# A spectral, spiking and mixture-of-experts layer on one core: synthesis loads moved ahead, block copies moved to GpSimd, one padding tile less

## The reference, cut to what matters

```python
x = x + conv(ln(x))        # spectral convolution on the sphere
t = t + shift_unit(ln(t))  # opcode unit: one-hot nibbles, shifts
x = x + spikes(ln(x))      # q, k, v through spiking neurons, linear attention, output projection
t = t + experts(ln(t))     # top 2 of 8 gated experts

def conv(x):               # x: 8 x 32 x 64 x 128, 32 latitudes as channels, 64 x 128 as the sphere
    xf = rfft(x) * (sqrt(2 pi) / 128)
    x_ft = einsum('lmj,bcjm->bclm', P_ANA, xf)
    top = einsum('bixy,ioxy->boxy', x_ft[:, :, :32, :32], w1)   # w1, w2 complex, 32 x 32 x 32 x 32
    bot = einsum('bixy,ioxy->boxy', x_ft[:, :, -32:, :32], w2)
    g = einsum('lmj,bclm->bcjm', P_SYN, concat(top, bot)) / sqrt(2 pi)
    return irfft(g) * 128
```

## Time and profile before

| what | us |
|---|---|
| median of 3 runs | 1301.36 |
| lowest, highest | 1296.43, 1301.63 |
| the profiled execution's own time | 1295.22 |
| its span | 1293.4 |
| busy: PE, DVE, ACT, POOL | 993.2, 859.4, 654.1, 564.4 |

### The profile page before, as it was taken

One profiled execution on the slowest core, in us unless ns is written; L12 is line 12 of the kernel. 1 busy time (PEld: TensorE's weight loads), 2 busy tenths in 40 slices (PEclk: granted clock), 3 DMA queues, 4 the chain that ended last, 5 costly groups with the idle time before them and its releaser, 6 DMA issues. The chain is left out here.

```text
span 1293.4 us, 23831 instructions
## 1 busy us (share of the span) xinstructions
PE 993.2 (77%) x6645; PEld 837.2 (65%) x6646; DVE 859.4 (66%) x2743; ACT 654.1 (51%) x1400; POOL 564.4 (44%) x731
## 2 busy tenths in 40 slices
PE   9847746876677675867666453099999999999997
PEld 7837644654456464746555342088888888888886
DVE  7707633756579898888984765066766766667665
ACT  3427732454868877687755431044444444444443
POOL 3310000121132575656665667535555555555554
PEclk9978977976878978778787655599999999999999
DMA  9997966940010010000000001111111111111110
GB/s 264 227 248 156 240 171 157 271 103 20 20 50 20 20 47 19 30 16 20 25 12 30 22 19 35 60 33 35 42 46 50 48 50 42 46 48 47 49 37 2
DMA packets 111924, 93.12 MB, mean 72 GB/s; under 512 B 8012, under 2 KB 100556, under 8 KB 111081
## 3 DMA queue, kind: packets, MB, share of 16 engines
q1 hardware_dynamic: 83753, 62.28, 20.5%
q0 software_dynamic: 9088, 17.33, 4.1%
q10 hardware_dynamic: 19008, 12.59, 3.8%
HBM read 55.61 MB, written 38.39 MB: 73 GB/s over the span
## 5 line engine op out<-in xcount | busy, mean ns | idle before, releaser
L1721 POOL DMA_INDIRECT out_dram<-res,index x156 | 155.8, 999 | 217.8 <-DVE res L1787 189.8
L1830 ACT ACTIVATE sil<-ps_h 128x512 f32<-128x512 f32 x156 | 93.1, 597 | 254.8 <-PE ps_h L1882 254.8
L1752 DVE TENSOR_TENSOR act_rows<-ps_h,sil 128x512 f32<-128x512 f32 x156 | 108.0, 692 | 133.4 <-ACT sil L1830 133.4
L1901 PE MATMUL ps_y<-r_raw,aT 128*128 x1248 | 164.8, 275 | 0.0
L1901 PEld LDWEIGHTS ps_y<-r_raw,aT 128*128 128x128 f32 x1248 | 151.6, 192 | 0.1
L160 POOL DMA_INDIRECT slots<-x_sb,r_pos x128 | 129.3, 1010 | 47.7 <-issue 36.0
L1880 PE MATMUL ps_h<-r_raw,uTh 128*128 x312 | 137.6, 441 | 1.6 <-DVE uTl L1746 1.6
L1881 PE MATMUL ps_h<-r_raw,uTh 128*128 x312 | 124.7, 400 | 0.0
L1882 PE MATMUL ps_h<-r_raw,uTl 128*128 x312 | 123.0, 394 | 0.0
L1092 PE MATMUL ps_q<-wqkv,zT 128*128 128x256 f32 x256 | 114.1, 537 | 0.0
L1204 POOL TENSOR_TENSOR x_sb<-x_sb,sy 128x256 f32<-128x256 f32 x64 | 43.8, 684 | 137.1 <-ACT sy L1340 136.9
(11 more groups left out here) (242 smaller groups left out, 2468.7 us busy)
## 6 DMA issues: line engine op xcount, KB each, us to landing
slots<-zero SPq DMA_DIRECT2D x4, 2652.0 KB, 23.2
pay<-slots SPq DMA_DIRECT2D x39, 272.0 KB, 2.8
coefc<-coefficients ACTq DMA_DIRECT2D x16, 256.0 KB, 6.2
mixed<-mo ACTq DMA_DIRECT2D x16, 256.0 KB, 9.1
gin<-mixed SPq DMA_DIRECT2D x16, 256.0 KB, 14.7
r_raw<-in_L_ffn_W SPq DMA_DIRECT2D x8, 508.0 KB
out_dram<-res,index POOLq DMA_INDIRECT x156, 2.2
pana<-in_legendre_analysis SPq DMA_DIRECT2D x1, 2048.0 KB, 12.8
```

Of the source, the lines that this page charges most:

```text
L1721: nc.gpsimd.indirect_dma_start(out_rows, bass.IndirectOffsetOnAxis(at, 0), res[:, m % RES, :], None, bounds_check=TOKENS - 1, oob_is_err=F ...
L1752: nc.vector.tensor_tensor(act_rows[:, k], ps_h[:, k, :, DFF:], sil[:, k], ALU.mult).then_inc(s_act, 1)
L1830: nc.scalar.activation(sil[:, k], ps_h[:, k, :, 0:DFF], ACT.Silu).then_inc(s_sil, 1)
L1901: ins = nc.tensor.matmul(dst, aT[:, k, (2 * e + h) * P:(2 * e + h + 1) * P], raw[:, 4 + h, col], start=(h == 0), stop=(h == 1))
```

## The change

It has four parts.

1. In the mixing block GpSimd does the plain copy of the upper half for every degree, with a semaphore `s_sp` of its own; PE and the coefficient loads wait for it too. ACT keeps the negated and the swapped copy.
2. `lw`, `psyn` and `gin` are loaded in the mixing block. They are allocated on the other side of SBUF (`late`), and `gin` now lies in the first slot of `wc`, which is free after chunk 5. SP issues `lw` and `psyn` behind the last late weights, waits for six chunks to be multiplied and stored and loads their degrees of `gin` (rows 0 to 23 of each group of 32, four transfers), waits for all stores and loads the rest (rows 24 to 31, four transfers). The first Legendre product waits for all of `gin`.
3. `pay` is cut in two; at the end of the spike stage `gap_of(6)` and the first part stand ahead of `route_deviation(7)`.
4. The expert stage works through `USED_TILES` = 155 tiles: the last turn has 11.

```diff
+USED_TILES = NTILES + PAIRS - 1
...
-        wc = sb("wc", [P, WS, O, LW, M], at=both)
+        wc = sb("wc", [P, WS, O, LW, M], at=late, side="right")
...
+            psyn = sb("psyn", [P, M, P], at=late, side="right")
+            lw = sb("lw", [P, 4, C], at=late, side="right")
+            gin = wc[:, 0].rearrange("p o l m -> p (o l m)").rearrange("p (j r m o) -> p j r m o", j=4, r=RB, o=16)
...
+            EARLY = 6
+
+            def load_mixed(eng, l0, l1, s):
+                for op in range(2):
+                    for half in range(2):
+                        p0 = op * 64 + half * L2
+                        src = mixed[op].rearrange("l (j h r) f -> h l j (r f)", j=4, h=2)[half, l0:l1]
+                        eng.dma_start(gin[p0 + l0:p0 + l1].rearrange("p j r m o -> p j (r m o)"), src).then_inc(s, 16)
...
                     for n in range(WS * LW // LQ, NCH):
                         sp.wait_ge(s_mm, n - WS * LW // LQ + 1)
                         load_late(sp, n)
-
+                    sp.dma_start(lw[:, :, :], t["L1_conv_lin_w"].rearrange("i d c -> d i c")).then_inc(s_load, 16)
+                    sp.dma_start(psyn[:, :, :], t["legendre_synthesis"].rearrange("p (m q) -> p m q", m=M)).then_inc(s_psyn, 16)
+                    sp.wait_ge(s_mm, EARLY)
+                    for k in range(2):
+                        sp.wait_ge(s_mw[k], STORED * EARLY // 2)
+                    load_mixed(sp, 0, EARLY * LQ, s_gin[0])
                     for k in range(2):
                         sp.wait_ge(s_mw[k], STORED * NCH // 2)
+                    load_mixed(sp, EARLY * LQ, L2, s_gin[1])
...
                     nc.gpsimd.memset(sblk[:, 1], 0.0).then_inc(s_zero, 1)
+                    pool.wait_ge(s_zero, 2)
+                    for n in range(NCH):
+                        k = n % 2
+                        pool.wait_ge(s_cc[k], n // 2 * 32 + 32)
+                        need(pool, s_mm, n - 1)
+                        for l in range(LQ):
+                            dst = sblk[64:96, k, l, :, RB:2 * RB].rearrange("p (q m) f -> p q m f", q=M // MQ)
+                            ins = nc.gpsimd.tensor_copy(dst, coefc[64:96, k, :, l])
+                            if l % 2:
+                                ins.then_inc(s_sp, 1)
...
                         need(act, s_sa, 2 * (n - 1))
+                        need(act, s_sp, 2 * (n - 1))
...
-                            nc.scalar.activation(dst[0:32], src, ACT.Copy)
...
                         pe.wait_ge(s_sa, 2 * n + 1)
+                        pe.wait_ge(s_sp, 2 * n + 1)
...
-                sp.dma_start(lw[:, :, :], t["L1_conv_lin_w"].rearrange("i d c -> d i c")).then_inc(s_load, 16)
-                sp.dma_start(psyn[:, :, :], t["legendre_synthesis"].rearrange("p (m q) -> p m q", m=M)).then_inc(s_psyn, 16)
                 sp.dma_start(einv[:, :], t["fourier_inverse"]).then_inc(s_einv, 16)
-                for j in range(4):
-                    for op in range(2):
-                        for half in range(2):
-                            src = mixed[op].rearrange("l (j h r) f -> j h l (r f)", j=4, h=2)[j, half]
-                            p0 = op * 64 + half * L2
-                            sp.dma_start(gin[p0:p0 + L2, j].rearrange("p r m o -> p (r m o)"), src).then_inc(s_gin[j], 16)
...
                 pe.wait_ge(s_psyn, 16)
+                pe.wait_ge(s_gin[0], 16 * 4)
+                pe.wait_ge(s_gin[1], 16 * 4)
                 for n in range(M):
                     j, at = n // (M // 4), n % (M // 4)
-                    if at == 0:
-                        pe.wait_ge(s_gin[j], 16 * 4)
...
                 add_output(pool, NP2 - 1, LAST)
+                gap_of(pool, NP2 - 2)
+                pay_power(pool, NP2 - 2)
                 route_deviation(pool, NP2 - 1)
-                gap_of(pool, NP2 - 2)
-                pay(pool, NP2 - 2)
+                pay_shares(pool, NP2 - 2)
                 scatter(pool, NP2 - 2, 0, NT)
...
-                    for m in range(STEPS):
+                    for m in range(STEPS - SPARE if last else STEPS):
```

More of the change, by code:

```diff
@@ L106, in build, with sb @@
     with ExitStack() as ctx:
-        def sb(name, shape, dt=F32, at=ctx):
-            return at.enter_context(nc.sbuf_tensor(name, shape, dt))
+        def sb(name, shape, dt=F32, at=ctx, side=None):
+            return at.enter_context(nc.sbuf_tensor(name, shape, dt, side=side))
         def pb(name, shape, dt=F32, at=ctx):
@@ L125, in build @@
         s_par = sem("norm_parameters_loaded")
-        mixed = spectral_conv(nc, t, sb, pb, sem, x_sb, ident, minus_half, x_view, routing, par_rows, s_par)
+        late = ExitStack()
+        mixed, loaded = spectral_conv(nc, t, sb, pb, sem, x_sb, ident, minus_half, x_view, routing, par_rows, s_par, late)
         routing.allocate(sb)
         with ExitStack() as a:
-            weights = synthesis_and_weights(nc, t, sb, pb, sem, ident, minus_half, a, mixed, par_rows, s_par, routing)
+            weights = synthesis_and_weights(nc, t, sb, pb, sem, ident, minus_half, a, loaded, par_rows, s_par, routing)
+            late.close()
             opcode_and_spikes(nc, t, sb, pb, sem, x_sb, ident, minus_half, weights, slots, routing)
@@ L414, in spectral_conv @@
             s_sa = sem("m_upper_blocks")
+            s_sp = sem("m_upper_plain_rows")
             s_mh = sem("m_first_degrees_mixed")
@@ L548, in _ @@
                         pe.wait_ge(s_sa, 2 * n + 2)
+                        pe.wait_ge(s_sp, 2 * n + 2)
                         need(pe, s_ea, n)
                         half_mixed(n, 1).then_inc(s_mm, 1)
-    return mixed
+    return mixed, (psyn, lw, gin, s_psyn, s_gin, s_load)
 def split3(nc, chain, parts, x, rest):
@@ L561, in split3, with synthesis_and_weights @@
     return nc.vector.tensor_tensor(parts[2], rest, parts[1], ALU.subtract)
-def synthesis_and_weights(nc, t, sb, pb, sem, ident, minus_half, keep, mixed, par_rows, s_par, routing):
+def synthesis_and_weights(nc, t, sb, pb, sem, ident, minus_half, keep, loaded, par_rows, s_par, routing):
+    psyn, lw, gin, s_psyn, s_gin, s_load = loaded
     wqkv = sb("wqkv", [P, 3 * C], at=keep)
@@ L1209, in gap_of, with pay_power @@
             nc.gpsimd.tensor_tensor(gap[:, :], top[:, 1], top[:, 0], ALU.subtract).then_inc(s_gap, 1)
-        SHARE_LINKS = 5
+        SHARE_LINKS, POWER_LINKS = 5, 3
         def pay(pool, v):
+            pay_power(pool, v)
+            pay_shares(pool, v)
+        def pay_power(pool, v):
             chain = Chain(pool, s_share, v * SHARE_LINKS)
@@ L1223, in pay, with pay_shares @@
             chain.link(nc.gpsimd.tensor_tensor(share[:, 0, :], total[:, :], inverse[:, :], ALU.pow))
+            assert chain.n == POWER_LINKS
+        def pay_shares(pool, v):
+            chain = Chain(pool, s_share, v * SHARE_LINKS + POWER_LINKS)
             chain.link(nc.gpsimd.tensor_tensor(share[:, 1, :], power[:, :], share[:, 0, :], ALU.mult))
@@ L1229, in pay @@
                 .then_inc(s_paid, 1)
-            assert chain.n == SHARE_LINKS
+            assert chain.n == SHARE_LINKS - POWER_LINKS
         def deviation(pool, n):
@@ L1629, in experts @@
     TURNS = SLOT_TILES // STEPS
+    SPARE = SLOT_TILES - USED_TILES
     out_rows = out.rearrange("b h w c -> (b h w) c")
@@ L1735, in _ @@
                 turn(TURNS - 1, last=True)
-                for m in range(3):
-                    scatter(TURNS, m - 3)
+                for m in range(USED_TILES - 3, USED_TILES):
+                    scatter(*divmod(m, STEPS))
             @block.vector
@@ L1812, in _ @@
                 turn(TURNS - 1, last=True)
-                for m in range(2):
-                    first_part(TURNS, m - 2)
-                    result(TURNS, m - 2)
+                for m in range(USED_TILES - 2, USED_TILES):
+                    first_part(*divmod(m, STEPS))
+                    result(*divmod(m, STEPS))
             @block.scalar
@@ L1932, in _ @@
                 turn(TURNS - 1, last=True)
-                n = SLOT_TILES
+                n = USED_TILES
                 at_out = [pe.snap(r, min_val=0, max_val=(E - 1) * C) for r in behind]
-                turn_gated(n - 1, 1)
-                expert_out(n - 2, 0, at_out[4:6])
-                expert_out(n - 1, 1, at_out[6:8])
+                turn_gated(n - 1, (n - 1) % 2)
+                for m in (n - 2, n - 1):
+                    q = m % G
+                    expert_out(m, m % 2, at_out[2 * q:2 * q + 2])
 _CONSTANTS = spectral_tables()
```

15 lines of the change are left out of this document (6 added, 9 removed).

## The result

The kernel after takes 1314.46 us (median of 4 executions, 1313.28 to 1315.43); the kernel before, timed beside it, 1299.85 (1296.43 to 1301.63). The ratio is 1.0124, 95% interval 1.0097 to 1.0151: slower by 16 us, 13 to 20 (the two medians lie 14.6 apart). The forecast was 1311.5 us, 10.3 more than before, with 14 of them from the moved loads. The profiled execution of after took 1315.43 us with a span of 1313.5.

What follows compares the result with a forecast made beforehand. Barrier-closed stages bound the kernel one behind another; mixing ends on weight transfers, synthesis waits on loads. Moved loads +14, powers -1, tile -2.7, copies hidden: +10.3 on 1301.4, some 1311.5 us; range 1293 to 1318.

Steps and rivals of the forecast that it cites:

- the base of the sum, 1301.4: Whole kernel before: median of its three runs, 6.1 us above the profiled execution, to which +10.3 was added.
- the term of +14: Synthesis loads moved into the mixing stage: first Legendre product at 216.3 instead of 202.4; term range -4 to +17.
- so 193: End of mixing: chunk 7's store lands 9.1 us after 184, with SP's last four transfers issued by then.
- the 197.8: Mixing stage: 24-row transfers end at 196.5, plus 1.3 us for chunk 7's store; the last four follow.
- 216.3: Start of synthesis: the 8-row transfers, 1.05 MB at 57 GB/s, take 18.5 us and release the first Legendre product.
- Rivals 1 and 2: Synthesis loads: few-row transfers run as fast as 32-row ones, 1294.7, chance 0.2; engine count limits, 1302.5, chance 0.18.
- costed at nothing (+1, hidden by part 2): GpSimd's plain copies in mixing: relieving ACT gains nothing, stage +1 us (-1 to +7), hidden by the moved loads.
- the 29 feared: Mixing stage: 32 POOL copies of 0.9 us, each holding DVE throughout, add 29 us to DVE's 54.3.
- Rival 3: Mixing stage: POOL's copies stretch it until it is DVE's, chunk 7 up to 7 us later, 1316; chance 0.1.
- Part 3, forecast -1: End of spike stage: powers ahead of the last deviation bring scatters 4.1 us earlier, less +2 and +1; range -3.5 to 0.
- the forecast of +2 and +1: End of spike stage: two more scatters under DVE's wide subtractions cost +2; last payload beside DVE's placing +1.
- Part 4, forecast -2.7: Expert stage: dropping the padding tile saves one PE tile period, -2.7 us (-2.5 to -3).

Runs made afterwards that it cites:

- the second: The kernel before, unchanged, profiled once more beside the others: 1299.51 us, ratio 0.9996 (0.9985 to 1.0008).

## Why the prediction was right, and what was mis-sized

**The direction, the place and the mechanism** were as forecast: PE's first Legendre product waits for the 8-row transfers, chunk 7 stays (171.46 against 171.44), a tile of the experts goes. Only the DMA share was read otherwise than forecast: 0.5 to 0.6 and not near 1, with 57 to 70 GB/s where 50 to 60 were expected. The time fell 3 us above the forecast, in its range. The change itself cost 16 us (13 to 20) and not 10.3; that the time came so near owes a part to the base of the sum, 1301.4, which lay above the later medians of the same kernel.

**Part 2, the term of +14, measured +18.3 between the profiles and +20 (15 to 25) alone.** Its steps:
- The table was expected in by 178; issued at 165.33, it landed 12.5 us later, at 178. The 24-row transfers had 170 GB/s forecast, 167 measured (window 184 to 188).
- The step that failed is the landing of chunk 7's store: "so 193", from a median of 9.1 us, which mixes stores beside the weights (7.8 to 10.7 us) with two on idle engines (2.6). It took 17.6 us, to 199.9. The sum had given the store its 1.3 us of DMA time, and not seen that it would land only when SP's early transfers are nearly through. The last four loads wait for it: +2 us on the 197.8 at which they were to start. The kernel with the table alone moved shows the other side, 2.6 us for the same store.
- From the issue of the last four to the first product it took 20.8 us (199.93 to 220.69) and not 18.5. At 57 GB/s their 1.05 MB need 18.4; the rest is probably the way of the first packets (no byte moves from 200 to 201 us) and the 0.13 MB of the inverse Fourier table, which share the engines. No run separates the two. With the store's 2 us that makes 220.7 where the sum had 216.3.
- The first profile of before had its product at 202.40, later than the second (199.88), because chunk 7 ran slowly and its weights came late. That hid some 2 us of the loss in the comparison of the two profiles: against the second one it is 20.8 us.

**Rivals 1 and 2 are out.** Few rows are not as fast as 32, and the number of engines is not it: 8 engines moved 57 GB/s to 8 rows side by side and 196 to 210 to 8 rows spread out, 16 engines 110 GB/s to 16 rows. The Trainium skill's rule in SBUF — State Buffer, Door 1: The DMA port swizzle, by which a transfer reaches only the ports on which its partitions lie, at some 27 GB/s each, is borne out in all five cases. Estimates from that figure, with the measured rates beside them: 8 ports for 32 rows (218, 227 measured), 6 for 24 (163, 167), 4 for 16 (109, 110), 2 for 8 (54, 57 to 63), and 8 for the spread ones (218, 196 to 210). The Trainium skill's rule in DMA: Bandwidth & Descriptors, Why a DMA increments its semaphore by 16 and not by 1, is seen in the shares, 0.75 for 24 rows and 0.5 for 8: it decides how many engines are busy. That the busy ones then wait for the ports is the first rule's reading; what the runs show is 7 GB/s from each of the eight with the rows side by side and 25 with them spread. The forecast had expected a share near 1 for 8 rows, though its own second rival named the eight engines.

**Part 1, costed at nothing (+1, hidden by part 2).** A copy took 0.73 us, where 0.9 was the estimate. DVE lost 10.5 us and not the 29 feared, and had the room. Rival 3 is out. Alone the part measured -1 us (-3 to +1): it is not shown to be a gain. If it is one, it may come by way of the clock in chunk 7, which the forecast did not have.

**Part 3, forecast -1, measured -1.9.** The first scatter comes 5.1 us earlier (13.4 instead of 18.5 us behind the last addition) and not 4.1: gap and powers took 4.9 us in their new place, beside DVE's statistics, instead of 6.06 beside its placing, so the deviation came 0.5 us later and not 1.7. The price was near the forecast of +2 and +1: the scatters lie under DVE's wide subtractions (+1.7 us), and the last payload takes 1.5 us more.

**Part 4, forecast -2.7, measured -3.0** in the pair of profiles and -2.6 in the median.

**The execution that the sum starts from.** Forecast on the median of before, 1301.4; the later medians of the same kernel are 1299.0 to 1300.8. Of the 16 us of the ratio the parts alone explain 20 - 1 - 2 - 2.6 = 14, within their intervals.

## What to carry to other kernels

Before moving a load ahead, see how many rows it fills and where they lie: cutting it by rows, to start with what is ready, can cost more than the idle time it fills, while cutting it across the free dimension keeps the rate. Move first what depends on nothing (the constant table, 6 us here), and look at what else must land while it runs: a small store on another queue may come in only behind it. Compare more than one profiled execution before explaining a few microseconds in code that was not touched.

## What the runs showed of the hardware that was not expected

- A store of 0.5 MB on ACT's queue, 2.6 us to land alone, took 16.7 to 18.6 us beside transfers of 16 or 24 rows from SP's queue. In two of these three kernels the issue of its second half held ACT's sequencer, for 7.5 and 5.3 us, in the third not. Whether the store waits for an engine or for the ports was not separated.
- The rate goes by the breadth on which the rows lie and not by their number: 8 rows, four apart, 196 to 210 GB/s; side by side, 57 to 63.
- A GpSimd copy of 32 rows by 512 elements takes 0.73 us beside DVE's, and stretches DVE's negated copies from 0.28 to 0.41 us in the mean.
- At the end of the mixing stage PE's granted clock fell behind its longer idle stretches: before chunk 6 with the copies (6.6 to 7.0 us idle), mostly before chunk 7 without them (2.1 to 3.8 us idle, five of six executions). With 1.54 to 2.49 us idle behind a chunk 6 in one piece it stayed at 1.00.
- The same program's stretch from synthesis to the end of the spikes, each engine's busy time equal within 2 us, took 557 us in one execution and 565 in another.
